# Query-weight load and fold in four pieces, and one layer-norm step placed earlier, in a one-core Perceiver layer

## The chip, the cores and the metric

One core of one Trainium2 chip runs the whole program. The metric is the device time of one execution in microseconds (us); lower is better. TensorE (PE) does matrix products, VectorE (DVE) and ScalarE (ACT) work on elements, GpSimd (POOL) on elements as well, and SyncE (SP) issues DMAs. Each engine runs its own list of instructions in order and waits on semaphores.

## The reference

```python
# x: 16 x 64 x 256, context: 16 x 1601 x 256
x = x + cross_attention(layernorm(x), ctx, seg_id)      # latent keys and values, 16 heads, rope
x = x + self_attention(layernorm(x))
x = x + moe(layernorm(x))                               # 8 routed experts (top 2) and 2 shared ones

# in cross_attention, what the change touches:
kv_c   = kv @ W_kvc                                     # 64 wide
q_c    = layernorm(x) @ W_dq                            # 96 wide
q_nope = (q_c @ W_uq).reshape(b, lq, H, HD)             # HD = 128
k_nope = (kv_c @ W_uk).reshape(b, lk, H, HD)
scores = q_nope . k_nope + rope(q_c @ W_qr) . rope(kv_c @ W_kr)
good   = (k_ids <= seg_id) & (k_ids >= seg_id - 8)
```

## The kernel before, in words

The 1024 rows of x are eight tiles of 128 rows (two batch elements each). Cross attention runs over the tiles in a software pipeline, then self attention, then the experts. What the change touches lies in the setup, the first 25 us, and what follows it is a long stretch that PE fills.

**Folding.** Instead of expanding queries and keys to 128 per head, the kernel multiplies W_uq and W_uk of each head into one 96 x 64 matrix (`w_q[:, 0]`). PE does it once, in the loop of L1592 and L1593, 16 matrix products that the profile shows as 32, since a product of 32-bit numbers takes two passes. Before it PE runs nine products on zeros (`keep_warm`, L1321) and a small fold of two products (L1589). The weights come in one transfer of 1280 KB, L362, third in SP's list; behind it stand the two context transfers of tile 0 (L367) and the rope weights `w_q[:, 1]` (L371). SP's transfers share the 16 DMA engines with those that ACT issues: x tiles 0 and 1, the constants `consts_a`, and the segment numbers `seg_i` (L1030 to L1032).

**Tile 0 behind the fold.** On PE: the transposes of the normed rows `xT(0)` (L1316, `ps<-consts_a,xn`), `kv(0)` (L1337), `qc(0)` (L1331), one tiny product for a flag (L1602), the rope query product `y_rope(0)` (L1345, which waits for `qc_done`) and `y_lat(0)`. On DVE: `query_compressed(0)` (L623) copies the result of `qc(0)` and signals `qc_done`; L729 makes the flag `far_i`, which every engine reads before a branch (`general`, L333 to L335); `front_k(0)` (L599 to L619) and `front_rotate(0)` (L605 to L607) apply rope. The fold's result is copied by ACT (L1040). The branch guards a general path that these inputs don't take.

**The window.** On POOL three long operations, L501, L503 and L504, turn the segment numbers into the attention window `win`. They begin when DVE has converted `seg_i` (L721 to L725), and `win` is wanted only at the scores of tile 0.

**The second rows.** `normed` (L591 to L595) writes the normed rows of one tile into the single buffer `xn`: it waits for `rstd` from POOL and until PE has transposed the rows that stood there before (`xT_ps`), and runs one tensor_scalar, L594. For tile 1 it stands at L798, behind the copy `front_qt(0)` (L636) and a wait for the rest of x. PE's transposes of tile 1 wait for it. Places in the order of each engine are set by the order in which the code is written; there is no scheduler.

Of the kernel before, what the change touches and what calls it, by code (L numbers as in the profile page):

```python
# [22 lines left out]
B, LQ, D = 16, 64, 256  # L23
# [5 lines left out]
H, HD, KVC, QC, R = 16, 128, 64, 96, 64  # L29
# [63 lines left out]
def build(nc, dram):  # L93
    with ExitStack() as ctx:
        def sb(name, shape, dt=F32):
            return ctx.enter_context(nc.sbuf_tensor(name, shape, dt))

        def sem(name):
            return ctx.enter_context(nc.semaphore(name))
# [24 lines left out]
        w_shared = sb("w_shared", [P, NSH, WX])  # L124
        w_routed = sb("w_routed", [P, E, WX])

        def carve(store):

            at = [0]

            def cut(*shape):
                n = int(np.prod(shape))
                part = store[:, at[0]:at[0] + n]
                at[0] += n
                letters = "abcd"[:len(shape)]
                return part.rearrange(f"p ({' '.join(letters)}) -> p {' '.join(letters)}",
                                      **dict(zip(letters[1:], shape[1:])))
            return cut


        cut = carve(w_shared[:].rearrange("p e n -> p (e n)"))
        w_uq, w_uk, w_uv, w_o = cut(H, QC), cut(H, KVC), cut(H, KVC), cut(H, D)

        cut = carve(w_routed[:, E // 2:, :].rearrange("p e n -> p (e n)"))
        w_q = cut(2, H, KVC)[0:QC]
# [20 lines left out]
        xn = sb("xn", [P, D])  # L166
# [102 lines left out]
        names = """seg_moved tiles_sent flag_set flag_ps far_ready g_step moe_in zero_set zeroed ws_in wr_in late_in c_xn3 c_xT_ps c_xT lg_ps lg e_done  # L269
# [6 lines left out]
        xs_in = [sem(f"xs_in{q}") for q in range(3)]  # L276
        b_up_in = [sem(f"b_up_in{q}") for q in range(2)]
        b_dn_in = [sem(f"b_dn_in{q}") for q in range(2)]
        names = """wu_in wr_q_in seg_in const_in x0_in x_in wk_in wv_in wo_in aw_in ctx_in win_ready dve_step pool_step
            absorb_q_ps absorb_q absorb_k_ps absorb_k absorb_m_ps absorb_m  # L280
            mv_ready rstd_ready xn_ready xT_ps xT_done qc_ps qc_done kv_ps kv_raw ylat_ps qlat
            yrope_ps yrope_used qrope krope kT_ps kT_done qt_lo_ps qt_lo qt_hi_ps qt_hi kvx
# [1 line left out]
            bxn bT_ps bxT_done bq_ps bqm bkv_ps bk_done bv_done bs_ps bs_used bmax bsub bp_done bpt_ps  # L284
            bpt_done bo_ps bon bot_done bproj_ps x3_done out_done""".split()
        S = {n: sem(n) for n in names}

        (wu_in, wr_q_in, seg_in, const_in, x0_in, x_in, wk_in, wv_in, wo_in, aw_in, ctx_in, win_ready, dve_step, pool_step,
         absorb_q_ps, absorb_q, absorb_k_ps, absorb_k, absorb_m_ps, absorb_m,
         mv_ready, rstd_ready, xn_ready, xT_ps, xT_done, qc_ps, qc_done, kv_ps, kv_raw, ylat_ps, qlat,  # L290
         yrope_ps, yrope_used, qrope, krope, kT_ps, kT_done, qt_lo_ps, qt_lo, qt_hi_ps, qt_hi, kvx,
# [1 line left out]
         bxn, bT_ps, bxT_done, bq_ps, bqm, bkv_ps, bk_done, bv_done, bs_ps, bs_used, bmax, bsub, bp_done, bpt_ps,  # L293
         bpt_done, bo_ps, bon, bot_done, bproj_ps, x3_done, out_done) = [S[n] for n in names]

# [56 lines left out]
        def after(eng, s, count):  # L352

            if not isinstance(count, int) or count > 0:
                eng.wait_ge(s, count)
# [3 lines left out]
        def _(sp):  # L359
            sp.dma_start(w_kT[:], dram["w_kT"]).then_inc(wk_in, 16)  # L360
            sp.dma_start(w_kd[:], dram["w_kd"]).then_inc(wk_in, 16)
            sp.dma_start(w_shared[:].rearrange("p e n -> p (e n)")[:, 0:H * (QC + KVC)], dram["w_uqk"]).then_inc(wu_in, 16)  # L362

            def load_ctx(i):
                after(sp, kv_ps, i)
# [37 lines left out]
            n = NU * D // ZC  # L403
# [155 lines left out]
        def _(dve):  # L559
# [31 lines left out]
            def normed(i, count, dst, used_sem, signal, used):  # L591
                dve.wait_ge(rstd_ready, count)
                after(dve, used_sem, used)
                dve.tensor_scalar(dst[:], x_sb[:, i, :], mv[:, i, 0:1], rstd[:, bass.ds(i, 1)],  # L594
                                  ALU.subtract, ALU.mult).then_inc(signal, 1)  # L595
# [25 lines left out]
            def query_compressed(i):  # L621
                dve.wait_ge(qc_ps, i + 1)
                dve.tensor_copy(qcT[:], ps[0:QC, 1, 0:P]).then_inc(qc_done, 1)  # L623
# [70 lines left out]
            def body(i, link_, behind, more):  # L694
                maxima(i, 0)
                query_compressed(i + 1)
                if more:
                    link_(dve.bn_stats(bn[:], x_sb[:, i + 2, :]))
                divided(i, 0, link_)
                if more:  # L700
                    link_(dve.bn_aggr(mv1[:], bn[:]))
                    dve.tensor_tensor(mv[:, i + 2, :], mv1[:], eps[:], ALU.add).then_inc(mv_ready, 1)
                front_k(i + 1, link_)
                front_rotate(i + 1)
                maxima(i, 1)
                front_rotated(i + 1)
                if not behind:
                    for j in range(2):
                        dve.wait_ge(absorb_m_ps, j + 1)
                        dve.tensor_copy(w_m[:, 2 * j:2 * j + 2, :].rearrange("p j d -> p (j d)"), ps[:, 4 + j, :]).then_inc(absorb_m, 1)  # L710
                divided(i, 1, link_)
                front_qt(i + 1)
                if more:
                    normed(i + 2, 3 if isinstance(i, int) and i == 0 else 2 * i + 2, xn, xT_ps, xn_ready, i + 2)
                if behind:
                    residual(i - 1, link_)
# [6 lines left out]
            link(dve.tensor_scalar(far[:, NT:2 * NT], seg[:], 0.0, None, ALU.is_lt))  # L723
            dve.tensor_reduce(far_n[:], far[:], AX.X, ALU.max).then_inc(flag_set, 1)
            dve.tensor_scalar(seg[:], seg[:], -LOOKBACK / 2, None, ALU.add).then_inc(seg_moved, 1)  # L725

            query_compressed(0)
            dve.wait_ge(flag_ps, 1)
# [66 lines left out]
            general(dve, g_tile, None, g_clear)  # L795
            front_qt(0)
            dve.wait_ge(x_in, 16)
            normed(1, 2, xn, xT_ps, xn_ready, 1)  # L798
            body(0, link, False, True)
            body(1, link, True, True)  # L800
            base = steps[0]
# [1 line left out]
            with dve.Fori(2, NT - 2) as i:  # L803
                n = [0]
# [50 lines left out]
            with dve.Fori(2, NT - 2) as i:  # L855
                n = [0]
# [150 lines left out]
            for m in range(MF + 1, MN):  # L1007
                product(m)
                t = m - MF
                if t >= IC + 1 and t % IC == 1:  # L1010
                    g = m // IC - 1
# [8 lines left out]
            g = len(PAIRS) - 1  # L1020
# [293 lines left out]
        def _(pe):  # L1314
# [273 lines left out]
            for k in range(KT):  # L1588
                last = pe.matmul(ps[:, 6, k * R:(k + 1) * R], w_kvcT[:, k * P:(k + 1) * P], w_kr[:], start=True, stop=True)  # L1589
            last.then_inc(absorb_k_ps, 1)  # L1590
            pe.wait_ge(wu_in, 16)
            for h in range(H):  # L1592
                last = pe.matmul(ps[0:QC, 4 + h // 8, (h % 8) * KVC:(h % 8 + 1) * KVC], w_uq[:, h, :], w_uk[:, h, :],  # L1593
                                 start=True, stop=True)
            last.then_inc(absorb_q_ps, 1)
# [329 lines left out]
def laid_out(inputs):  # L1925

    a = {k: np.asarray(v) for k, v in inputs.items()}
    g = lambda n: a["L0_xattn_" + n]
    s = lambda n: a["L0_attn_" + n]
    rows = lambda w: w.reshape(KT, P, -1).transpose(1, 0, 2)  # L1930
    heads = lambda w, n: w.reshape(n, H, HD).transpose(2, 1, 0)

    def expert(gate, up, down):

        n = gate.shape[0]
        gu = np.stack([gate, up], 1).transpose(0, 3, 1, 2).reshape(n, KT, P, 2 * I).transpose(0, 2, 1, 3)
        dn = down.transpose(0, 2, 1).reshape(n, IC, P, D).transpose(0, 2, 1, 3)
        return np.concatenate([gu.reshape(n, P, -1), dn.reshape(n, P, -1)], 2)

    flat = lambda w: np.ascontiguousarray(w).reshape(w.shape[0], -1)  # L1940
    c = constants()
    c["w_router"] = flat(rows(a["L0_ffn_w_router"].T))
    pack = lambda table: np.concatenate([c[n] for n in table], 1)
    a_wo = s("Wo").reshape(NP_, 2, DH, D).transpose(0, 2, 1, 3).reshape(P, 2, D)
    return {
        "x": a["x"].reshape(T, D),
        "ctxT": a["ctx_2048"].transpose(0, 2, 1),
        "seg": a["itok_BxS_0_1023"].reshape(NT, P).T,
        "consts_a": pack(PACK_A), "consts_b": pack(PACK_B),
        "rope_c_all": c["rope_c_all"], "rope_s_all": c["rope_s_all"],  # L1950
        "w_uqk": np.concatenate([flat(heads(g("W_uq"), QC)), flat(heads(g("W_uk"), KVC))], 1),
        "w_uvo": np.concatenate([flat(heads(g("W_uv"), KVC)), flat(g("W_o").reshape(H, HD, D).transpose(1, 0, 2))], 1),
        "w_kT": np.concatenate([g("W_kvc").T, g("W_kr")], 1),
        "w_kd": np.concatenate([rows(g("W_kvc")), np.zeros((P, KT, R), np.float32), rows(g("W_dq"))], 2),
        "w_qr": g("W_qr").reshape(QC, H, R),
        "a_w": np.concatenate([flat(rows(s("Wq"))), flat(rows(s("Wk"))), flat(rows(s("Wv"))), flat(a_wo)], 1),
        "w_routed": expert(*(a["L0_ffn_" + n] for n in ("wg", "wu", "wd"))),
        "w_shared": expert(*(a["L0_ffn_" + n] for n in ("sg", "su", "sd"))).transpose(1, 0, 2),
    }
# [18 lines left out]
```

## Time and profile before

| what | value |
|---|---|
| three runs | 514.43, 515.78, 516.9 us (median 515.78) |
| profiled execution | 515.22 us |
| its span in the trace | 513.4 us |
| granted TensorE clock | full in all 40 slices |
| PE busy | 496.7 us, 97% of the span |
| DVE, ACT, POOL busy | 246.8, 184.9, 67.7 us |

The profiled execution took 1.8 us more than its span, which is what lies before the first and behind the last recorded instruction. PE is nearly always busy from 24 us on, so the time is to be found in the few places where PE waits; many of them lie in the setup.

### The profile page before, as it was taken

To read this page: it belongs to the slowest core of one execution; us is meant where nothing else is said; L and a number is where in the kernel's file an instruction comes from. 1 tells how busy PE (TensorE), PEld (TensorE's weight loads), DVE (VectorE), ACT (ScalarE), POOL (GpSimd) and SP (SyncE) were. 2 spreads that over 40 slices of the span, in tenths; PEclk is the share of its full clock that TensorE was granted. 3 is DMA by queue.
4 is the path that set the end of the run, shared out by engine and by line. 5 is a ranking of instruction groups with operands and counts; after the bars stand their busy time and mean duration, and the time that the engine had idled before them with its cause. 6 is when DMAs were issued, how large, how long until landed. Compare 5 with 4: busy or idle time off the path is not lost.

```text
span 513.4 us, 10570 instructions
## 1 busy us (share of the span) xinstructions
PE 496.7 (97%) x3878; PEld 361.3 (70%) x3878; DVE 246.8 (48%) x547; ACT 184.9 (36%) x533; POOL 67.7 (13%) x74
## 2 busy tenths in 40 slices
PE   7799999999999999998999998999999999999997
PEld 6476876876877788886788885555555555556886
DVE  1485776776766678888562221212222222222334
ACT  1367566566666544444411111212212112111110
POOL 6200000000000112132006500000000000000650
PEclk9999999999999999999999999999999999999999
DMA  7730000001990019300614162787887877852341
GB/s 224 274 138 21 1 22 20 0 20 60 357 419 4 2 41 431 146 0 1 263 48 133 72 250 67 268 289 262 317 272 270 320 262 282 311 197 83 84 121 41
DMA packets 24456, 82.05 MB, mean 160 GB/s; under 512 B 2881, under 2 KB 16513, under 8 KB 20321
## 3 DMA queue, kind: packets, MB, share of 16 engines
q1 hardware_dynamic: 21392, 73.30, 39.6%
q0 software_dynamic: 1536, 4.20, 2.6%
q10 hardware_dynamic: 1488, 4.00, 2.1%
q8 instruction: 28, 0.46, 0.3%
q14 instruction: 12, 0.09, 0.1%
HBM read 73.10 MB, written 8.39 MB: 159 GB/s over the span
## 4 chain that ended last, share of the span: by engine, by line
PE 87%; DVE 5%; issue 3%; DMA 2%; ACT 1%; POOL 0%; DVEq 0%; SPq 0%; POOLq 0%
PE ps L1812 17%; PE ps L1720 13%; PE ps L1316 12%; PE ps L1836 9%; PE ps L1732 6%; PE ps L1395 5%; PE ps L1345 5%; PE ps L1364 5%; PE ps L1487 3%; PE ps L1383 3%; DMA w_shared<-in_w_uqk 2%; PE ps L1497 1%; PE ps L1676 1%; PE ps L1337 1%; PE ps L1360 1%
## 5 line engine op out<-in xcount | busy, mean ns | idle before, releaser
L1812 PE MATMUL ps<-w_routed,xnT 128*64 x320 | 93.8, 436 | 1.6 <-DVE x_sb L969 1.6
L1720 PE MATMUL ps<-xT_all,w_shared 128*128 128x256 f32 x320 | 75.6, 380 | 0.0
L1812 PEld LDWEIGHTS ps<-w_routed,xnT 128*64 128x64 f32 x320 | 42.0, 137 | 38.4 <-issue 27.2
L1720 PEld LDWEIGHTS ps<-xT_all,w_shared 128*128 128x128 f32 x320 | 60.4, 190 | 8.3 <-issue 0.4
L1093 ACT ACTIVATE w_routed<-ps,neg_top 128x128 f32<-128x128 f32 x128 | 45.0, 378 | 15.9 <-DVE neg_top L644 15.9
L1836 PE MATMUL ps<-w_routed,hidT 128*64 x200 | 47.4, 384 | 0.0
L1812 PE MATMUL ps<-w_shared,xnT 128*64 128x384 f32 (+1 forms) x160 | 46.9, 436 | 0.0
L1812 PE MATMUL ps<-x_up,xnT 128*64 128x384 f32 (+1 forms) x160 | 46.9, 436 | 0.0
L1316 PEld LDWEIGHTS ps<-consts_a,w_routed 128*128 128x128 f32 x336 | 37.2, 141 | 13.5 <-issue 10.4
L1285 ACT COPY hidT<-ps 128x384 f32<-128x384 f32 x20 | 9.6, 479 | 100.7 <-PE ps L1316 100.7
L1258 ACT ACTIVATE sil<-ps 128x256 f32<-128x256 f32 x40 | 15.3, 384 | 84.3 <-PE ps L1720 84.2
L1316 PE MATMUL ps<-consts_a,w_routed 128*128 128x128 f32 x336 | 44.3, 276 | 1.1 <-DVE w_routed L831 0.5
L1836 PEld LDWEIGHTS ps<-w_routed,hidT 128*64 128x64 f32 x200 | 25.8, 137 | 15.0 <-issue 3.3
L1364 PEld LDWEIGHTS ps<-hid,w_routed 128*128 128x128 f32 x256 | 33.6, 192 | 1.2
L963 DVE COPY hidT<-ps 128x256 f32<-128x256 f32 x20 | 8.5, 425 | 53.4 <-PE ps L1316 53.4
L1364 PE MATMUL ps<-hid,w_routed 128*128 128x128 f32 x256 | 33.7, 275 | 0.0
L554 POOL DMA_INDIRECT x_up<-y_slots,slot_i x8 | 8.0, 995 | 182.7 <-DVE hidT L876 180.5
L644 DVE TENSOR_REDUCE neg_top<-ps 128x4 f32<-128x512 f32 x32 | 22.0, 689 | 16.5 <-PE ps L1364 16.0
L493 POOL TENSOR_TENSOR rstd<-mv,half 128x1 f32 (+1 forms) x16 | 9.1, 566 | 157.7 <-DVE mv L574 95.9
L1345 PE MATMUL ps<-w_routed 96*128 96x512 f32 x64 | 29.0, 595 | 0.3 <-issue 0.3
L1395 PE MATMUL ps<-w_routed 128*128 128x256 f32 x128 | 29.0, 379 | 0.0
L1093 ACT ACTIVATION_READ_ACCUMULATOR w_routed<-ps,neg_top 128x1 f32 x128 | 27.8, 217 | 0.0
(180 smaller groups left out, 873.6 us busy)
## 6 DMA issues: line engine op xcount, KB each, us to landing
w_routed<-in_w_routed SPq DMA_DIRECT2D x8, 1920.0 KB, 14.4
x_up<-in_w_routed SPq DMA_DIRECT2D x10, 1280.0 KB, 5.9
w_shared<-in_w_routed SPq DMA_DIRECT2D x10, 1280.0 KB, 6.4
b_down<-in_w_routed SPq DMA_DIRECT2D x10, 640.0 KB, 5.6
w_shared<-in_w_routed SPq DMA_DIRECT2D x10, 640.0 KB, 5.3
w_shared<-in_w_shared SPq DMA_DIRECT2D x1, 3840.0 KB, 12.0
w_shared<-in_w_uvo ACTq DMA_DIRECT2D x1, 2560.0 KB, 12.6
x_slots<-sil SPq DMA_DIRECT2D x16, 160.0 KB, 2.2
```

Source lines behind the costliest of these rows:

```text
L644: dve.tensor_reduce(neg_top[:, b, n], s[:, n], AX.X, ALU.min).then_inc(top_ready, 1)
L1093: last = act.activation(Pb[:, b, n, :], s[:, n, :], ACT.Exp, scale=-1.0, bias=neg_top[:, b, n:n + 1], accum_out=sums[:, b, n:n + 1])
L1316: return pe.transpose(out, src, ident[:])
L1345: last = pe.matmul(ps[:, 2 * part + c, :], qcT[:], w[:, c * 512:(c + 1) * 512], start=True, stop=True)
L1364: last = pe.matmul(at[:, n * P:(n + 1) * P], QT[:, b, h:h + 2, :], KTb[:, b, :], start=False, stop=n == 3)
L1383: last = pe.matmul(ps[KVC * h:KVC * h + KVC, 4 + 2 * b, :].rearrange("p (j t) -> p j t", t=P), kv_ext[:, b, 0:KVC], PT[:, b].rearrange("p ...
L1395: last = pe.matmul(ps[:, b, 0:D], UT[:, j, h, :], w_m[:, 2 * j + h, :], start=j == h == 0, stop=j == NP_ // 2 - 1 and h == 1)
L1487: last = pe.matmul(ps[:, b, g * P:(g + 1) * P], w[:, k, g * P:(g + 1) * P], xnT[:, k, :], start=k == 0, stop=k == KT - 1)
L1720: last = pe.matmul(ps[:, UP_BANK[m], half_ * D:(half_ + 1) * D].rearrange("p (n t) -> p n t", n=2), w_shared[:, j, at:at + P], xT_all[:, i ...
L1732: last = pe.matmul(ps[:, Y_BANK[g][n], n * D:(n + 1) * D], hidT_ring[m % 4][:, n * P:(n + 1) * P], w_shared[:, PAIRS[g][0], GU + c * D:GU ...
L1812: last = pe.matmul(ps[rows, b, 0:hi - lo], xnT[:, k, rows], w, start=k == 0, stop=k == KT - 1)
L1836: last = pe.matmul(ps[rows, 6, 0:D], hidT[:, c, rows], w, start=c == 0, stop=c == IC - 1)
```

## The change

The weights W_uq and W_uk are laid out in memory head by head, 96 and then 64 numbers for each head, so that a quarter of the buffer holds both factors of four heads. SP issues four transfers of 320 KB in place of the one, each with a semaphore of its own, and PE waits for one of them before every fourth head. On DVE `normed` of tile 1 moves from L798 to just before `query_compressed(0)`. The wait for the rest of x stays where it was. Each row of a transfer has 2560 bytes in place of 10240.

```diff
-        w_uq, w_uk, w_uv, w_o = cut(H, QC), cut(H, KVC), cut(H, KVC), cut(H, D)
+        w_uqk, w_uv, w_o = cut(H, QC + KVC), cut(H, KVC), cut(H, D)
+        w_uq, w_uk = w_uqk[:, :, 0:QC], w_uqk[:, :, QC:]
...
+        wu_in = [sem(f"wu_in{q}") for q in range(4)]
...
-            sp.dma_start(w_shared[:].rearrange("p e n -> p (e n)")[:, 0:H * (QC + KVC)], dram["w_uqk"]).then_inc(wu_in, 16)
+            for q in range(4):
+                part = slice(q * (H // 4) * (QC + KVC), (q + 1) * (H // 4) * (QC + KVC))
+                sp.dma_start(w_shared[:].rearrange("p e n -> p (e n)")[:, part], dram["w_uqk"][:, part]).then_inc(wu_in[q], 16)
...
             dve.tensor_scalar(seg[:], seg[:], -LOOKBACK / 2, None, ALU.add).then_inc(seg_moved, 1)
+            normed(1, 2, xn, xT_ps, xn_ready, 1)
 
             query_compressed(0)
...
             dve.wait_ge(x_in, 16)
-            normed(1, 2, xn, xT_ps, xn_ready, 1)
             body(0, link, False, True)
...
-            pe.wait_ge(wu_in, 16)
             for h in range(H):
+                if h % (H // 4) == 0:
+                    pe.wait_ge(wu_in[h // (H // 4)], 16)
                 last = pe.matmul(ps[0:QC, 4 + h // 8, (h % 8) * KVC:(h % 8 + 1) * KVC], w_uq[:, h, :], w_uk[:, h, :],
                                  start=True, stop=True)
...
-        "w_uqk": np.concatenate([flat(heads(g("W_uq"), QC)), flat(heads(g("W_uk"), KVC))], 1),
+        "w_uqk": flat(np.concatenate([heads(g("W_uq"), QC), heads(g("W_uk"), KVC)], 2)),
```

PE's list at the fold, before. `w_shared` is the buffer in which the two factors lie, `w_kT` the small fold's, and the names in brackets are the semaphores waited for.

```order
L1589 MATMUL ps<-w_kT 128x64 [waits wk_in]
L1589 MATMUL ps<-w_kT 128x64
L1593 MATMUL ps<-w_shared 96x64 [waits wu_in]
L1593 MATMUL ps<-w_shared 96x64 x15
L1316 MATMUL ps<-consts_a,xn 128x128 [waits xn_ready,const_in]
L1316 MATMUL ps<-consts_a,xn 128x128
```

The same place of PE's list after the change (lines are four or five further down in this file).

```order
L1593 MATMUL ps<-w_kT 128x64 [waits wk_in]
L1593 MATMUL ps<-w_kT 128x64
L1598 MATMUL ps<-w_shared 96x64 [waits wu_in0]
L1598 MATMUL ps<-w_shared 96x64 x3
L1598 MATMUL ps<-w_shared 96x64 [waits wu_in1]
L1598 MATMUL ps<-w_shared 96x64 x3
L1598 MATMUL ps<-w_shared 96x64 [waits wu_in2]
L1598 MATMUL ps<-w_shared 96x64 x3
L1598 MATMUL ps<-w_shared 96x64 [waits wu_in3]
L1598 MATMUL ps<-w_shared 96x64 x3
L1320 MATMUL ps<-consts_a,xn 128x128 [waits xn_ready,const_in]
L1320 MATMUL ps<-consts_a,xn 128x128
```

One wait for everything has become four waits with four heads behind each; nothing else moves on PE.

DVE's list where the compressed query of tile 0 is copied, before. `seg` holds the segment numbers, L623 is `query_compressed`, L729 the flag.

```order
L724 TENSOR_REDUCE far_n<-far 128x1 [waits dve_step]
L725 TENSOR_SCALAR seg<-seg 128x8
L623 COPY w_routed<-ps 96x128 [waits qc_ps]
L729 TENSOR_SCALAR far_i<-ps 1x1 [waits flag_ps]
L599 TENSOR_TENSOR hidT<-w_routed,consts_a 128x2x64 [waits kv_raw]
```

And after, where L598 is the tensor_scalar of `normed`:

```order
L728 TENSOR_REDUCE far_n<-far 128x1 [waits dve_step]
L729 TENSOR_SCALAR seg<-seg 128x8
L598 TENSOR_SCALAR xn<-x_sb,mv,rstd 128x256 [waits xT_ps,rstd_ready]
L627 COPY w_routed<-ps 96x128 [waits qc_ps]
L734 TENSOR_SCALAR far_i<-ps 1x1 [waits flag_ps]
L603 TENSOR_TENSOR hidT<-w_routed,consts_a 128x2x64 [waits kv_raw]
```

The tensor_scalar stands ahead of the copy of the compressed query, of the flag and of the rope work, and it waits for PE's transposes of tile 0.

## Rows read from the trace of the kernel before

**Rows 1.** The page's part 4: who holds the chain that ended last.

```profile
PE 87%; DVE 5%; issue 3%; DMA 2%; ACT 1%; POOL 0%; DVEq 0%; SPq 0%; POOLq 0%
```

**Rows 2.** The chain in the first 40 us: start us, us, what.

```profile
1.99 8.10 DMA w_shared<-in_w_uqk
10.13 2.94 PE ps L1593 x32
15.54 1.97 PE ps L1345 x4
17.53 1.22 DVE w_routed L605
21.54 1.30 PE ps L1316 x10
24.00 0.42 DVE xn L594
24.50 0.41 PE ps L1316 x2
```

**Rows 3.** Timeline of the setup: start us, us, engine, line, operation [idle before].

```profile
7.04 0.17 DVE L721 CAST seg<-seg_i 128x8 f32<-128x8 int32 x1 [1.03 <-DMA seg_i<-in_seg]
7.85 0.66 PE L1589 MATMUL ps<-w_kT 64*128 64x64 f32 x4
9.88 1.89 POOL L503 TENSOR_TENSOR xT_all<-xT_all 128x1024 f32<-128x1024 f32 x1
11.87 3.65 POOL L504 TENSOR_SCALAR w_routed<-xT_all 128x1024 bf16<-128x1024 f32 x1
12.90 0.39 PE L1316 MATMUL ps<-consts_a,xn 128*128 128x128 f32 x2
15.15 0.29 DVE L623 COPY w_routed<-ps 96x128 f32<-96x128 f32 x1 [7.38 <-PE ps L1331]
15.42 0.27 DVE L599 TENSOR_TENSOR hidT<-w_routed,consts_a 128x128 f32<-128x128 f32 x1
19.98 1.22 DVE L632 TENSOR_TENSOR w_routed<-w_routed 128x1024 f32<-128x1024 f32 x1
22.86 1.23 DVE L636 COPY w_routed<-ps 128x1024 f32<-128x1024 f32 x1 [1.65 <-PE ps L1316]
```

**Rows 4.** DMAs issued at 1.75, 2.94 and 3.46 us: issue to landing, last column.

```profile
seg_i<-in_seg ACTq DMA_DIRECT2D x1, 4.0 KB, 5.3
w_routed<-in_ctxT SPq DMA_DIRECT2D x1, 128.0 KB, 8.4
w_routed<-in_w_qr SPq DMA_DIRECT2D x1, 384.0 KB, 8.9
```

**Rows 5.** DMA traffic from 3 to 4 us, then 7 to 8 us.

```profile
DMA packets 220, 0.37 MB, mean 367 GB/s; under 512 B 26, under 2 KB 120, under 8 KB 220
...
DMA packets 41, 0.42 MB, mean 420 GB/s; under 512 B 0, under 2 KB 0, under 8 KB 0
```

**Rows 6.** DMA queues from 6 to 7 us: packets, MB, share of 16 engines.

```profile
q1 hardware_dynamic: 34, 0.35, 87.2%
q10 hardware_dynamic: 2, 0.00, 0.1%
```

**Rows 7.** DVE's tensor_scalar beside POOL, timeline at 177 and 233 us.

```profile
176.96 1.90 POOL L524 TENSOR_TENSOR w_routed<-w_routed,smx 128x1024 f32<-128x1024 f32 x1 [3.54 <-DVE smx L672]
178.36 0.65 DVE L594 TENSOR_SCALAR xn<-x_sb,mv,rstd 128x256 f32<-128x256 f32 x1
...
233.42 2.31 DVE L866 TENSOR_SCALAR x_up<-x_sb,mv,rstd 128x256 f32<-128x256 f32 x2
233.58 2.00 POOL L524 TENSOR_TENSOR w_routed<-w_routed,smx 128x1024 f32<-128x1024 f32 x1 [4.61 <-DVE smx L672]
```

**Rows 8.** Line L866 alone: ns min/median/max.

```profile
L866 DVE TENSOR_SCALAR x_up<-x_sb,mv,rstd x8: 404/406/1990, 233.4 to 248.6; 128x256 f32<-128x256 f32 x8
```

**Rows 9.** Line L335, the branch behind the flag, on PE, ns min/median/max.

```profile
L335 PEldq COMPARE_BRANCH  x1: 4832/4832/4832, 16.5 to 16.5; - x1
```

More of the change, by code:

```diff
@@ L278, in build @@
         b_dn_in = [sem(f"b_dn_in{q}") for q in range(2)]
-        names = """wu_in wr_q_in seg_in const_in x0_in x_in wk_in wv_in wo_in aw_in ctx_in win_ready dve_step pool_step
+        names = """wr_q_in seg_in const_in x0_in x_in wk_in wv_in wo_in aw_in ctx_in win_ready dve_step pool_step
             absorb_q_ps absorb_q absorb_k_ps absorb_k absorb_m_ps absorb_m
@@ L286, in build @@
         S = {n: sem(n) for n in names}
-        (wu_in, wr_q_in, seg_in, const_in, x0_in, x_in, wk_in, wv_in, wo_in, aw_in, ctx_in, win_ready, dve_step, pool_step,
+        wu_in = [sem(f"wu_in{q}") for q in range(4)]
+        (wr_q_in, seg_in, const_in, x0_in, x_in, wk_in, wv_in, wo_in, aw_in, ctx_in, win_ready, dve_step, pool_step,
          absorb_q_ps, absorb_q, absorb_k_ps, absorb_k, absorb_m_ps, absorb_m,
```

## The prediction

> **What bounds the kernel.** I read the chain of waits first, then its first 25 us in order of time, then the timeline of the engines there, and last the queues of the DMAs. PE holds 87% of the chain [rows 1], so what the setup wins or loses reaches the end almost undivided: from 24 us on every step hangs on an earlier one, and the later loads are issued by signals of that same work. In the setup the chain [rows 2] is: the weights landing at 10.09, the fold of 32 passes to 12.90, where the transposes of tile 0 begin, y_rope(0) at 15.54, rope on DVE from 17.53, PE again at 21.54, the norm of the second rows at 24.00 and its transposes at 24.50. The reader is to see that two pieces stand in the open: the fold behind the last byte, and the norm behind the copy L636.
>
> **The norm leaves its old place.** L636 runs from 22.86 for 1.23 us, to 24.09 [rows 3]; the transposes of tile 1 begin at 24.50 [rows 2]. Without L594 between them they begin some 0.05 us behind the copy, at 24.14. I take 0.36 us, with bounds 0.32 and 0.42 (the norm's own duration). PE goes on with the scores of tile 0, whose first half needs nothing later than that copy. The wait for the rest of x stays, and those rows are issued earlier if anything.
>
> **The fold, taken alone.** PE leaves the nine warm-up products at 7.85 and the small fold at 8.51 [rows 3], before which the first quarter can't start. The fold's pace is 2.77 us (10.13 to 12.90) for 32 passes, 0.087 each. Bound by PE it ends at 8.5 + 2.8 = 11.3. Bound by the landing it ends 8 passes, 0.7 us, behind the last quarter. That quarter lands at 10.09 if the size of a packet costs nothing. By the rows of mixed smaller packets, 367 GB/s against 420 with 10 KB ones [rows 5], 1.31 MB take 3.57 us in place of 3.12, so it lands at 10.5. The fold then ends between 10.8 and 11.3; I take 11.25, since PE is the later in both, and xT(0) begins 1.65 us earlier. Three more issues on SP, 0.5 us each as between those at 2.94 and 3.46 [rows 4], push the context and the rope weights back by 1.5 us in SP's list. They were queued behind the big transfer anyway: the context landed at 2.94 + 8.4 = 11.3 and is wanted at 11.45, the rope weights at 3.46 + 8.9 = 12.4 [rows 4] and are wanted near 13.9. If both slip by 1.5 us, kv(0) starts at 12.8 and 1.3 us of the 1.65 are gone, in the case where they would count.
>
> **What the new place costs.** The norm now stands ahead of query_compressed(0) on DVE. It is released when xT(0) ends, 0.39 us behind its start: at about 11.65. It looks free, as DVE idles 7.38 us before L623 [rows 3]. It is not free if POOL is in a long operation. In the trace DVE's tensor_scalar from buffer to buffer doesn't run beside one. At 178.36 it stood 0.65 us and ended at 179.01, while POOL's L524 ran to 178.86. At 233 us two of them took 2.31 us together, the longer 1.99 where the others take 0.41, and ended at 235.73 with L524 ending at 235.58 [rows 7, 8]. Both ended 0.15 us behind POOL. The Trainium skill says the same as a rule (SBUF — State Buffer, "Who interferes with whom"): VectorE in a two-port mode and GpSimd exclude each other for a whole instruction, and the first to issue holds the ports. This case's trace agrees, with 1.99 against 0.41 us, and the rule speaks against this place.
>
> Here POOL computes the window: L503 from 9.88 to 11.77, L504 from 11.87 for 3.65 us, to 15.52 [rows 3]. A norm released at 11.65 would wait out L503 and slip in before L504. One released after 11.87 waits for the end of L504, E, and ends at E + 0.15; L623 follows (0.29), then y_rope(0) 0.10 later as before (15.44 to 15.54): at E + 0.54. The flag and with it PE's branch, 4.83 us from 16.5 [rows 9], stand behind the same copy and move alike. So the question is when POOL starts. Its chain hangs on seg_i, which landed at 7.04, and L504 begins 4.83 us and ends 8.48 us after that landing. seg_i is 4 KB and took 5.3 us [rows 4]; from 6 to 7 us its queue moved its last 2 packets while the other queue moved 34 of 10 KB [rows 6]. One such packet holds an engine for about 16/41 = 0.39 us [rows 5]. With quarters the packets at the head are 2.5 KB, about 0.1 us each, so the stragglers should come sooner. Bounds for the landing are 6.0 (no packet of the big transfer in its way) and 7.1 (nothing gained). I take 6.55, midway but nearer the row's end than a full gain would be. L504 then runs from 11.4 to 15.0, and the norm, released at 11.65, is 0.25 us too late for the gap.
>
> **The sum.** y_rope(0) starts at 15.0 + 0.54 = 15.54, just where it did: the fold's 1.65 us are all spent in the wait. The 0.36 of the norm stay. From the profiled 515.22 us that is 514.9. The profiled execution lies 0.56 below the median 515.78; I start midway, at 515.5, and get 515.1. With seg_i landing from 6.0 to 7.1, E goes from 14.5 to 15.6, and the gain from 0.9 to -0.2: 514.6 to 515.7.
>
> **Rivals.**
> First, the norm slips in before L504. It does if seg_i still lands after about 6.85, or if the fold ends 0.25 us sooner. Then y_rope moves by the 1.65 us of the fold and the sum is 1.65 + 0.36 = 2.0: 513.5 us. For it speaks that the gap of the row before, 11.77 to 11.87, lies behind my 11.65; against it that four semaphores and a slower stream can only make PE later, and that seg_i should land sooner. The rope work L599 would then be due at 13.6, during L504. The row before can't say whether it would be held as well: it began at 15.42, 0.1 before POOL's end, and took its 0.27. If held, it ends 2 us later than due and rope on DVE (from 17.53, less 1.65) starts at 16.5 in place of 15.9. L632 ended at 21.20 and PE resumed at 21.54, so half of that is slack, and the gain is 1.7 to 2.0. The Trainium skill has that too (same page and section): with two SBUF inputs VectorE contends with a GpSimd instruction that reads SBUF. By it the rope work is held; no run here shows it yet.
>
> Second, POOL's L504 doesn't hold DVE at all, since the rows that show a hold are of another operation, L524, with two inputs. Then all is gained whatever seg_i does: 2.0 us, 513.5.
>
> Third, slower. L504 ends later than 15.4, because seg_i lands later than 6.9 and the norm misses the gap all the same, for a last quarter that lands after 10.7. Then y_rope starts at E + 0.54: at 16.06 with E as before, half a microsecond late, against 0.36 gained. That is 0.15 us lost; with seg_i at 7.5, half a microsecond behind its row, 0.6 lost: 515.6 to 516.1. For it: four transfers where there was one. Against it: smaller packets share an engine more evenly.
>
> Fourth, the weights in quarters land no sooner than the whole and the norm's old place was covered by something else (the second half of ACT's copy for the scores): nothing changes, 515.5.
>
> **How the numbers follow.** Forecast 0.50; the first rival 0.26; the second 0.08; the third 0.10; the fourth 0.06. The likeliest gives 515.1, its own range is 514.3 to 516.0 with the runs' scatter of a microsecond. The range reaches to the first two rivals: 513.0 to 516.2. This kernel's measurement can tell 0.5% from nothing, 2.6 us, a time under 513.2. Only the first two rivals come near, with 2.0 us; scatter carries them over in about 3 of 10 cases, 0.10, and 0.03 I add for a PE branch that ends sooner by a microsecond with x landed before it. Slower by 2.6 us nothing here reaches; 0.03 for what I have not seen. The same: 0.84.
>
> **What would show it.** The tensor_scalar L598 with a duration near 3 us and an end 0.15 us behind POOL's L504; seg_i's landing before 6.8; the fold ending near 11.3 without a wait between quarters; y_rope(0) within 0.5 us of 15.54; the transposes of tile 1 0.05 us behind the copy. L598 at 0.4 us with y_rope near 13.9 means the first or second rival, told apart by POOL's clock at that moment. A fold that ends after 12 makes the transfer's part of this wrong.

## The result, and the profile after

The changed kernel took 515.29 us (median of 21 runs, 512.07 to 516.48), the kernel before 517.59 us in 21 runs of the same series (514.02 to 522.35). The ratio is 0.9943, with a 95% interval from 0.9921 to 0.9965: 0.6% faster, 1.8 to 4.1 us. The kernel before had shown 515.78 in three runs; with more runs its median moved up by 1.8 us, over twice the 0.7 us that the change was forecast to bring. The profiled execution of the changed kernel took 514.32 us with a span of 512.5, 0.9 us less than before.

So there are two questions: why the setup became faster at all, where the forecast had let its gain vanish, and why the runs show more than the 0.9 us of the two profiles.

The chain of the changed kernel in the setup: start us, us, what ("issue" is time in which the engine waited for nothing that the profile shows).

```profile
3.42 7.41 DMA w_shared<-in_w_uqk
10.87 0.89 PE ps L1598 x8
11.76 0.23 PE ps L1320 x2
12.12 1.13 PE ps L1341 x8
14.23 1.97 PE ps L1349 x4
16.23 1.23 DVE w_routed L609
20.54 1.30 PE ps L1320 x10
23.23 0.41 PE ps L1320 x2
26.07 0.77 issue
27.23 0.89 PE ps L1341 x8
```

Against [rows 2]: y_rope(0) starts at 14.23 in place of 15.54, PE resumes behind the branch at 20.54 in place of 21.54, the transposes of tile 1 start at 23.23 in place of 24.50. The gain is 1.31, 1.00 and 1.27 us at these places. It is 0.9 at the end.

The timeline of the changed kernel, same columns as [rows 3]:

```profile
7.01 0.17 DVE L725 CAST seg<-seg_i 128x8 f32<-128x8 int32 x1 [0.97 <-DMA seg_i<-in_seg]
8.01 2.57 PE L1598 MATMUL ps<-w_shared 128*96 128x64 f32 x24
10.87 0.89 PE L1598 MATMUL ps<-w_shared 128*96 128x64 f32 x8 [0.29 <-DMA w_shared<-in_w_uqk]
11.60 0.39 PE L1320 MATMUL ps<-consts_a,xn 128*128 128x128 f32 x2
11.85 3.65 POOL L508 TENSOR_SCALAR w_routed<-xT_all 128x1024 bf16<-128x1024 f32 x1
12.10 0.94 DVE L598 TENSOR_SCALAR xn<-x_sb,mv,rstd 128x256 f32<-128x256 f32 x1 [4.35 <-PE ps L1320]
13.85 0.29 DVE L627 COPY w_routed<-ps 96x128 f32<-96x128 f32 x1 [0.81 <-PE ps L1335]
14.12 0.27 DVE L603 TENSOR_TENSOR hidT<-w_routed,consts_a 128x128 f32<-128x128 f32 x1
14.69 0.29 DVE L623 TENSOR_TENSOR hidT<-hidT,w_routed 128x128 f32<-128x128 f32 x1
```

The reader is to see the sixth row. The moved norm was released at 12.10, behind the start of POOL's window operation at 11.85, just as forecast. It was held, but for half a microsecond: 0.94 in place of 0.41 us. It ended at 13.04, 2.5 us before POOL's row does, and left DVE idle for 0.81 us before the copy of the compressed query. The last two rows, rope work with two inputs, ran inside POOL's operation at their usual 0.27 and 0.29.

### The profile page after: what moved, and what is told of

Its sections match the earlier page's. It is cut to its first block, busy times and chain, and to the rows that moved or that the text cites. A ratio compares the mean times of both kernels' runs of the same rounds, so it can differ in the third digit from the quotient of the medians.

```text
span 512.5 us, 10574 instructions
## 1 busy us (share of the span) xinstructions
PE 496.6 (97%) x3878; PEld 361.1 (70%) x3878; DVE 247.4 (48%) x547; ACT 185.1 (36%) x533; POOL 67.6 (13%) x74
## 4 chain that ended last, share of the span: by engine, by line
PE 87%; DVE 6%; issue 3%; DMA 1%; ACT 1%; SPq 0%; POOL 0%; DVEq 0%; POOLq 0%
PE ps L1817 17%; PE ps L1725 13%; PE ps L1320 12%; PE ps L1841 9%; PE ps L1737 6%; PE ps L1399 5%; PE ps L1349 5%; PE ps L1368 5%; PE ps L1491 3%; PE ps L1387 3%; DMA w_shared<-in_w_uqk 1%; PE ps L1341 1%; PE ps L1501 1%; PE ps L1681 1%; PE ps L1364 1%
```

## The experiments

The mean granted clock of each execution turned out to matter, so the table gives it for all kernels. "Full" are executions with a mean clock of at least 0.9985, "low" those of at most 0.9905. The three rows of the kernel before belong to the three groups of experiments below.

| kernel | runs | median | at full clock | low clock | ratio to before (95%) |
|---|---|---|---|---|---|
| before, first group | 29 | 517.20 | 514.75 (8 runs) | 11 | |
| before, second group | 35 | 517.05 | 514.44 (7) | 11 | |
| before, third group | 29 | 516.69 | 515.01 (8) | 11 | |
| the change | 21 | 515.29 | 512.71 (5) | 1 | 0.9943 (0.9921 to 0.9965) |
| e1_split | 12 | 514.95 | 513.59 (2) | 1 | 0.9938 (0.9907 to 0.9969) |
| e2_norm | 12 | 517.83 | 515.33 (1) | 6 | 1.0006 (0.9968 to 1.0043) |
| e4_late_aw | 12 | 514.95 | 512.95 (2) | 0 | 0.9942 (0.9909 to 0.9974) |
| e5_warm13 | 12 | 516.81 | 515.68 (6) | 1 | 0.9986 (0.9957 to 1.0014) |
| e6_fill | 12 | 515.64 | 515.46 (9) | 0 | 0.9975 (0.9945 to 1.0005) |
| e7_all_first | 12 | 518.30 | 514.92 (3) | 5 | 1.0015 (0.9977 to 1.0054) |
| e8_two | 12 | 515.03 | 513.71 (5) | 2 | 0.9962 (0.9928 to 0.9995) |
| e9_wide5 | 12 | 513.83 | 513.00 (3) | 2 | 0.9954 (0.9925 to 0.9983) |
| e10_wide5_fill2 | 12 | 513.48 | 513.04 (7) | 0 | 0.9949 (0.9922 to 0.9976) |
| e11_before_wide | 12 | 515.89 | 515.39 (5) | 2 | 0.9987 (0.9956 to 1.0018) |

### Each part alone: e1_split and e2_norm

e1_split is the change with this undone:

```diff
-            normed(1, 2, xn, xT_ps, xn_ready, 1)
 
             query_compressed(0)
...
             dve.wait_ge(x_in, 16)
+            normed(1, 2, xn, xT_ps, xn_ready, 1)
             body(0, link, False, True)
```

> The change with the second norm back in its old place, so only the four transfers are left. In the profile of the changed kernel xT(0) starts 1.3 us earlier (12.90 to 11.60), and y_rope(0) too. If the two parts add up: the transposes of tile 1 begin near 23.6 (before 24.50, changed 23.23), gain against the kernel before about 0.9 us less what PE gives back in its branch, 515.78 becomes some 515. If the norm was what held the gain back, this kernel would be faster than the changed one, with y_rope(0) before 14.2. If the whole 0.57% of the changed kernel comes from the transfers, the ratio is 0.994 here.

e2_norm is the kernel before with that edit alone, the other way round.

> The kernel before with the second norm alone moved. The weights land as before, xT(0) ends at 13.3, the norm is released during POOL's L504 (11.87 to 15.52). If POOL holds the ports to its end, as I predicted, the norm ends at 15.67, y_rope(0) starts at 16.06 in place of 15.54 and the kernel is 0.1 us slower. If the hold is shorter, as the changed kernel's 0.94 us suggests, the norm ends by 14.3, y_rope(0) stays at 15.54, the transposes of tile 1 come 0.3 to 0.4 us earlier, and the ratio is 0.999.

The transfers carry all that the runs can tell: 0.9938 alone, 0.9943 with the norm. The norm alone is at 1.0006. In its profile the moved norm ran inside POOL's operation and was not held at all:

```profile
13.35 3.66 POOL L504 TENSOR_SCALAR w_routed<-xT_all 128x1024 bf16<-128x1024 f32 x1
...
14.24 0.41 DVE L594 TENSOR_SCALAR xn<-x_sb,mv,rstd 128x256 f32<-128x256 f32 x1 [4.99 <-PE ps L1316]
```

By my forecast it would have waited to 17.16. It ended at 14.65. I had expected y_rope(0) at 15.54; it started at 16.37, since the weights, in one transfer as before, landed at 10.92 in this execution and not at 10.09. The profile of e1_split was the first with another clock. It has the times of the changed kernel up to y_rope(0) (14.12), and then, in PE's pause before the branch target, this (start:end, us, busy times with counts of PE, its weight loads, DVE, ACT and POOL, granted clock, DMA share, GB/s):

```profile
18.00:19.00 1.00, 0.00 (x0) 0.00 (x0) 0.96 (x2) 0.84 (x1) 0.00 (x0) 1.00 0.97 251
19.00:20.00 1.00, 0.00 (x0) 0.00 (x0) 0.79 (x1) 0.00 (x0) 0.00 (x0) 0.74 0.82 322
20.00:21.00 1.00, 0.79 (x4) 0.82 (x5) 0.00 (x0) 0.09 (x1) 0.00 (x0) 0.50 0.99 410
26.00:27.00 1.00, 1.00 (x8) 0.96 (x8) 0.21 (x1) 0.00 (x0) 0.00 (x0) 0.85 1.00 430
```

PE stands idle from 17.8; its clock goes to half, 1.2 GHz, during the 20th microsecond and is back near 26.3. Over the executions of the kernel before, a mean clock lower by 0.01 goes with 4.5 us more (fitted over 29 runs, 514.5 at full clock). Most of its scatter of 9 us goes with the clock, and that is the second thing in which the two kernels differ: 11 of 29 executions before are at low clock, and one of 21 after.

A mean clock is a sum over the whole execution, and it doesn't say where the clock fell. In this profile it fell at a second place, behind short pauses of PE (1.59 and 0.48 us, near 235 and 237 us), far from anything that the change touches:

```profile
237.00:238.00 1.00, 0.74 (x7) 0.74 (x8) 0.94 (x3) 0.69 (x2) 0.00 (x0) 0.97 0.00 0
238.00:239.00 1.00, 1.00 (x7) 1.00 (x6) 0.93 (x5) 0.11 (x1) 0.06 (x1) 0.50 0.00 0
```

The profiles of e5_warm13 and e8_two show a drop at the same place. So the mean of 0.989 of this execution has nothing to do with the fold.

### How long POOL holds: e3_probe

Sixteen more tensor_scalars on DVE, ahead of the moved norm, whose results are not used:

```diff
+            for _ in range(16):
+                link(dve.tensor_scalar(y_sb[:], x_sb[:, 0, :], 2.0, 1.0, ALU.mult, ALU.add))
             normed(1, 2, xn, xT_ps, xn_ready, 1)
```

> The changed kernel with 16 more tensor_scalars on DVE (256 columns, buffer to buffer, results unused) ahead of the second norm, so that one is always running or waiting from 7.8 us on, beside POOL's three window operations. If any POOL operation holds them for its whole length: one or two run at each seam between POOL operations, and the rest last 1.9 or 3.6 us. If the two-input tensor_tensors hold and the tensor_scalar with bf16 result does not: about 2 us each beside the first two, and 0.4 to 0.9 us beside the third, some six of them. If the hold is only the first microsecond of the third, one of 1 us and then 0.41 each.

Its timeline, POOL's three operations and five of the sixteen, each asked for in a window of its own:

```profile
7.65 1.90 POOL L505 TENSOR_TENSOR xT_all<-consts_a,seg 128x1024 f32<-128x1024 f32 x1 [1.72 <-DVE seg L729]
7.73 1.96 DVE L731 TENSOR_SCALAR y_sb<-x_sb 128x256 f32<-128x256 f32 x1
...
9.62 1.89 POOL L507 TENSOR_TENSOR xT_all<-xT_all 128x1024 f32<-128x1024 f32 x1
...
11.61 3.72 POOL L508 TENSOR_SCALAR w_routed<-xT_all 128x1024 bf16<-128x1024 f32 x1
...
11.70 1.10 DVE L731 TENSOR_SCALAR y_sb<-x_sb 128x256 f32<-128x256 f32 x1
...
13.16 0.29 DVE L731 TENSOR_SCALAR y_sb<-x_sb 128x256 f32<-128x256 f32 x1
...
14.47 1.00 DVE L731 TENSOR_SCALAR y_sb<-x_sb 128x256 f32<-128x256 f32 x1
15.83 0.29 DVE L731 TENSOR_SCALAR y_sb<-x_sb 128x256 f32<-128x256 f32 x1
```

Beside the tensor_tensor one tensor_scalar lasts as long as POOL's operation, 1.96 us, as in [rows 7]. Beside POOL's tensor_scalar with a bf16 result there are three stretches. From 11.70 to 12.80 DVE is held. From 12.83 to 14.43 five tensor_scalars run at 0.29 each. One that begins at 14.47 is held to 15.47, 0.14 us behind the end of POOL's row. I had expected a hold at the start or none, not the second one. With this the changed kernel's 12.10 to 13.04 is a release 1.19 us behind POOL's start, and the probe's was 1.19 as well (11.61 to 12.80). e2_norm fits: with an end no sooner than 13.35 + 1.19 = 14.54, the norm, begun at 14.24, took its usual 0.41 and ended at 14.65. Two more profiles measure the same holds on the norm itself. In e9_wide5 it began 0.57 us behind POOL's start, took 0.62 and ended again 1.19 behind it. In e7_all_first it began 0.45 us before POOL's end, in the second hold, and ended 0.16 behind it:

```profile
10.99 3.65 POOL L508 TENSOR_SCALAR w_routed<-xT_all 128x1024 bf16<-128x1024 f32 x1
14.19 0.61 DVE L598 TENSOR_SCALAR xn<-x_sb,mv,rstd 128x256 f32<-128x256 f32 x1 [7.29 <-PE ps L1320]
```

### The streaming of the fold: e7_all_first, e8_two

e7_all_first keeps layout, transfers and norm, but PE waits for all before the first head:

```diff
+            for q in range(4):
+                pe.wait_ge(wu_in[q], 16)
             for h in range(H):
-                if h % (H // 4) == 0:
-                    pe.wait_ge(wu_in[h // (H // 4)], 16)
```

> The changed kernel (four transfers, layout, norm moved), but PE waits for all four transfers before the first head. PE then pauses from 8.0 to 10.8 as in the kernel before, and the fold ends near 13.6. If the gain is the streaming of the fold, all of it is gone: xT(0) at 13.6, executions with a clock of 0.984 to 0.990 are back, median 517 to 518, ratio 1.000 to 1.002. If layout or smaller transfers gain by themselves, the ratio stays below 0.998.

No gain is left that the runs can tell: 1.0015, and 5 of 12 executions are at low clock again. Its profile has PE idle for 2.33 us, and the fold behind it:

```profile
7.97 0.66 PE L1593 MATMUL ps<-w_kT 64*128 64x64 f32 x4
10.95 2.90 PE L1598 MATMUL ps<-w_shared 128*96 128x64 f32 x32 [2.33 <-DMA w_shared<-in_w_uqk]
13.69 0.39 PE L1320 MATMUL ps<-consts_a,xn 128*128 128x128 f32 x2
```

e8_two has transfers of 12 and of 4 heads:

```diff
-            for q in range(4):
-                part = slice(q * (H // 4) * (QC + KVC), (q + 1) * (H // 4) * (QC + KVC))
+            for q, (lo_, hi_) in enumerate(((0, 12), (12, H))):
+                part = slice(lo_ * (QC + KVC), hi_ * (QC + KVC))
...
-                if h % (H // 4) == 0:
-                    pe.wait_ge(wu_in[h // (H // 4)], 16)
+                if h in (0, 12):
+                    pe.wait_ge(wu_in[h // 12], 16)
```

> The changed kernel with two transfers, of 12 heads and of 4, in place of four of 4. SP issues the context 0.95 us earlier than in the changed kernel (3.89), so that kv(0) waits less for it (12.12 there). The first transfer lands later, near 9.5, and PE folds 12 heads in 2.1 us: the fold ends near 12.3 if bound by that, against 11.6. If earlier landing of context matters more, xT(0) and kv(0) start before 11.9. Pause on PE from 8.0 to 9.5: by the clock theory some executions of 0.987 return. I expect 0.5 to 1.5 us slower than the changed kernel, ratio 0.996 to 0.998.

I was wrong on the landing. The fold ran without a pause from 8.82 to 11.75, so 12 heads had landed by 8.8 where I had said 9.5. The transposes of tile 0 began at 11.58 and kv(0) at 11.81 without a wait for the context, y_rope(0) at 14.22, the same as with four. Two transfers do the work of four in the setup. The intervals don't tell the two kernels apart; 513.71 against 512.71 at full clock rests on five runs each.

### Other loads out of the way: e4_late_aw

```diff
             load_ctx(1)
+            load_ctx(2)
             sp.dma_start(consts_b[:], dram["consts_b"]).then_inc(moe_in, 16)
             sp.dma_start(w_routed[:, E // 4, 0:4 * KT * D], dram["a_w"]).then_inc(aw_in, 16)
-            with sp.Fori(2, NT) as i:
+            with sp.Fori(3, NT) as i:
```

> The changed kernel with the constants for the experts and the self-attention weights (1.25 MB together, wanted at 150 us) issued behind the context of tile 2, near 28 us, in place of 16 us. In the changed kernel's profile PE's branch lasts 5.1 us and PE stands 0.77 us in the middle of qc(1), both at code loads. If these loads wait behind the weights' traffic, the branch shrinks by 0.3 to 1 us and the pause by up to 0.8: 0.5 to 1.5 us faster than the changed kernel. If the code load has its own pace, nothing changes.

0.9942 against 0.9943: no change that the runs can tell, though with intervals of 1.7 us to either side they don't exclude half a microsecond. In its profile PE resumed behind the branch at 20.02, with the other loads not yet issued (28.70); the branch lasted 4.75 us in place of 5.11, and the pause in qc(1) was gone. But e8_two, with the loads in their old place, has 4.85 us and no pause either. So nothing speaks for this traffic as the cause, and a small share of it stays open.

### Filling PE's pauses: e5_warm13, e6_fill

e5_warm13 is the kernel before with `WARM_UP = 13`.

> The kernel before with 13 warm-up products in place of 9, which fill PE's pause of 1.6 us between the small fold (8.51) and the weights (10.13) and end before the weights land. If the pause is why some executions of the kernel before have a mean granted clock of 0.984 to 0.990 (11 of 29, 519.3 to 522.5 us), those executions vanish, the median falls from 517.2 to about 515.5, and the fastest stay at 513.5 to 514.5. If the clock has nothing to do with that pause, the spread stays and the ratio is 1.000.

e6_fill is the changed kernel with six products on zeros:

```diff
             y_lat(0)
+            pe.wait_ge(far_ready, 1)
+            keep_warm(6)
```

> The changed kernel with six products on zeros behind y_lat(0), in PE's pause before the branch target (17.9 to 20.5). 13 of 21 executions of the changed kernel have a mean clock of 0.992 or 0.993 and 515.5 us, five have a full one and 512.7; in two profiles the clock drops to half at 19.3 or 19.7 us, in that pause. If the pause brings the drop, nearly all executions now have a full clock and the median is 512.8 to 513.3, ratio to the kernel before 0.991. If the filler only delays the branch, 0.5 to 2 us slower than the changed kernel. If the drop is not tied to pauses, no change.

Both did to the clock what the two expectations say that filled pauses would do: one low execution of 12 where the kernel before has a third, and nine of 12 at full clock where the changed kernel has five of 21. Both lost the time again at full clock: 515.68 against 514.44 in the same group, and 515.46 against 512.71. The profiles show one place. PE stops in the middle of a group of products, with nothing that it waits for. In e5_warm13, e6_fill and the changed kernel:

```profile
25.76 0.39 PE L1364 MATMUL ps<-hid,w_routed 128*128 128x128 f32 x2
27.32 0.83 PE L1364 MATMUL ps<-hid,w_routed 128*128 128x128 f32 x6 [1.17 <-issue]
```

```profile
24.01 0.94 PE L1368 MATMUL ps<-hid,w_routed 128*128 128x128 f32 x7
26.89 0.27 PE L1368 MATMUL ps<-hid,w_routed 128*128 128x128 f32 x1 [1.94 <-issue]
```

```profile
25.69 0.38 PE L1335 MATMUL ps<-xnT,w_kd 128*96 128x128 f32 x2
26.85 0.38 PE L1335 MATMUL ps<-xnT,w_kd 128*96 128x128 f32 x2 [0.77 <-issue]
```

The stop lies behind pass 2 of qc(1) in the changed kernel and in the one before. With four more products, that is eight passes, it lies eight passes earlier; with six more, twelve passes earlier. So it sits at a fixed distance from the start of PE's program, to within a pass (in e7_all_first it lies behind pass 1 of qc(1)). A queue of the kind "instruction" moved one packet of 0.02 MB two to three microseconds before it ended (24 to 25 us in the changed kernel, 25 to 26 before). I take it for a load of code; no run tests that. Its end is tied to the branch: in the seven profiles that show a stop it ended 6.0 to 6.6 us behind the moment when PE resumed at the branch target, and in e4_late_aw and e8_two, where PE came to the place 6.3 us or more behind that moment, there is none. So a PE that comes to the place sooner waits there the longer. Where the stop falls decides its price too. In the scores, DVE's maxima, ACT's exponentials and the copies of the keys behind them come later, and y_rope(1) with them.

### The same fill without more instructions: e9_wide5, e10_wide5_fill2, e11_before_wide

A product of 512 columns, the zeros read twice, fills twice the time in one instruction:

```diff
+            def keep_warm_wide(n, b=7):
+                for _ in range(n):
+                    pe.matmul(bank(b).rearrange("p (r t) -> p r t", r=2), zeros[:, 0:P],
+                              zeros[:, 0:2 * P].unsqueeze(1).to_broadcast([P, 2, 2 * P]), start=True, stop=True)
...
-            keep_warm(WARM_UP)
+            keep_warm(1)
+            keep_warm_wide(4)
```

This is e9_wide5. e10_wide5_fill2 adds `keep_warm_wide(2, 4)` behind `y_lat(0)`. e11_before_wide is the kernel before with `keep_warm(5)` and `keep_warm_wide(4)`.

> The changed kernel with the nine warm-up products of 256 columns as one of 256 and four of 512: the same columns in four instructions fewer. In the changed kernel's profile PE stands 0.77 us in the middle of qc(1), and with 4 or 6 more products (the two kernels with added fillers) it stands 1.17 and 1.94 us some 8 and 13 passes earlier in the program, ending near 26.9 to 27.3. If that pause is a load of code that falls at a fixed place of the program, it now falls 8 passes later, in or behind kv(1), and PE reaches it after 26.9: the pause is gone, 0.5 to 0.8 us faster than the changed kernel, 512.0 at full clock, median 514.6. If the pause is something else, no change. The scatter by the clock stays.

> The last kernel with two products of 512 columns on zeros behind y_lat(0), 1.7 us in PE's pause before the branch target (17.9 to 20.4), still two instructions fewer than the changed kernel. By both theories together (clock drops come from that pause, the code load falls at a fixed place): nearly all executions at full clock, the code pause no longer than 0.5 us and behind the scores, median 512.5 to 513.0, ratio 0.991, faster than both kernels. If the filler costs what the six did (515.5 at full clock), the code theory is wrong.

> The kernel before with warm-up of five products of 256 and four of 512 columns: the length of 13, which fills the pause before the weights, in the nine instructions of before. The one with 13 instructions had fewer slow-clock executions but was 1.2 us slower at full clock (515.7 against 514.5). If that was the code load moved into the scores, it is now gone: 514.5 at full clock, executions with a clock under 0.9905 (11 of 29 and 11 of 35 of the kernel before) nearly gone, median 515.0 to 515.8, ratio 0.996 to 0.997. If it stays at 515.7 at full clock, filling the pause costs time in another way.

e10_wide5_fill2 is faster than the kernel before (0.9949, interval 0.9922 to 0.9976), as the change is. Its filler covers the pause, and the clock stays:

```profile
17.37 1.72 PE ps L1329 x4
19.09 0.77 issue
19.86 1.30 PE ps L1320 x10
...
25.18 0.44 PE ps L1340 x4
25.61 0.22 PE ps L1346 x2
25.84 0.21 issue
26.05 0.94 PE ps L1346 x6
```

The load of code now costs 0.21 us and falls behind pass 2 of kv(1), four passes later than in the changed kernel, as two products fewer ask for. No execution had a mean clock under 0.995, and the range is the narrowest of all, 512.7 to 515.5. At full clock it stands at 513.04 against the change's 512.71, so the shift of the code load didn't show as a gain there; nor did it in e9_wide5 (513.00), where I had expected 512.0. The profile of e9_wide5 has no stop, but its clock fell at 20.4 us, so PE came to the place late anyway. Both ratios lie inside the change's interval, and the kernels ran on different chips: that it beats the change is not shown.

e11_before_wide gave a part of what I expected. At full clock it took 515.39 us and not 514.5, which is 0.4 more than the kernel before in the same group (515.01), where e5_warm13 had 1.2 more; the median, 515.89, and the ratio, 0.9987, missed my ranges, and 2 of 12 executions were low. With five to eight executions at full clock on a side I can't tell what is left from nothing. Its profile shows the pause before the weights from the inside. The warm-up ended at 8.44, only 0.6 us later than before (e5_warm13: at 9.17). Its products on 256 columns fell from 0.63 to 0.38 us already between 4 and 5 us, in e5_warm13 between 5 and 6. So the pause was not filled, and this is what it can cost (columns as above; then the chain):

```profile
10.00:11.00 1.00, 0.45 (x5) 0.45 (x6) 0.00 (x0) 0.00 (x0) 1.00 (x1) 1.00 0.76 143
11.00:12.00 1.00, 1.00 (x10) 1.00 (x8) 0.00 (x0) 0.00 (x0) 0.92 (x2) 0.53 0.22 74
12.00:13.00 1.00, 1.00 (x8) 1.00 (x8) 0.00 (x0) 0.00 (x0) 1.00 (x1) 0.50 0.01 4
```

```profile
10.55 4.97 PE ps L1599 x32
15.52 0.43 PE ps L1316 x2
```

PE had waited 1.45 us for the weights. The clock fell to half at about 11.1, half a microsecond behind the start of the fold, and the fold took 4.97 us where it takes 2.94 at full clock [rows 2]. The transposes of tile 0 began 2.6 us later than in [rows 3]. In the same profile it fell a second time, near 24.7, at the pause before the branch target. Two drops in one execution gave the mean clock of 0.99 here, as two drops at other places gave 0.989 in e1_split. This is the one profile with a drop at the fold.

## Why the prediction was right, and where it was not

The range, 513.0 to 516.2, holds the time, and so does the range of the likeliest case. Most of the chance was on a difference too small to tell, and the measured one is at that bound: 0.6% where I had drawn it at 0.5%. That 515.1 lies so near the measured 515.29 is luck. I started from 515.5 where the kernel before has 517.59, 2.1 us too low, and forecast a gain of 0.4 where 2.3 were measured, and the two errors cancel. The mechanism of the forecast is wrong in one step and lacks another.

**The norm, 0.36 us.** Its transposes began 0.14 us behind the copy, not 0.05: 0.27 us gained. Right in kind; e2_norm can't tell it from nothing. What was gained there seems to be lost again a little later: from PE's restart behind the branch to the stop in qc(1) the changed kernel took 5.53 us in place of 5.81, but the stop ended 6.31 behind the restart in place of 6.14.

**The fold, 1.65 us.** The last quarter landed at 10.83, where I had said 10.5 at the latest, and PE waited 0.29 us for it. My 10.5 started from one landing, 10.09. In the other profiles with a single transfer it came at 9.91, 10.51 and 10.92, and the last of four quarters at 10.07 to 10.86 in all. So the quarters cost nothing that these profiles can tell, and my row was an early one. xT(0) began at 11.60, 1.30 us earlier and not 1.65. The context made kv(0) wait to 12.12; it was queued 1.4 us later, as said. It cost no more, since ACT's copy of the folded weights stood in the way as well.

**"Waits for the end of L504, E, and ends at E + 0.15".** This is the step that failed. The release came behind the start of L504, as forecast, though seg_i landed at 7.0 and not at 6.55. (DVE took up seg_i at 7.04, 8.34, 8.51 and 8.70 in the profiles with one transfer, at 5.87 to 7.23 in those with two or four: that it comes sooner with smaller transfers was right, and again my row was an early one.) But L504 is no L524. The rows that I had were all of a tensor_tensor, and there the hold lasts to the end. e3_probe shows two holds of 1.1 and 1.0 us with 1.6 us free between them. The moved norm lost 0.5 us, all of it in DVE's idle time, and y_rope(0) moved by 1.31 us. In e6_fill the norm was released at 11.76, ahead of POOL's start at 12.07, and y_rope(0) came at 14.22 all the same: the hold cost nothing. The second rival, "L504 doesn't hold DVE at all", comes nearest, and had 0.08. The rule of the Trainium skill that I named (SBUF — State Buffer, "Who interferes with whom"), that the first to issue holds the ports for the whole instruction, agrees with [rows 7] and not with e3_probe; here the measurement decides. The same page's second rule, that two SBUF inputs contend with a GpSimd instruction that reads SBUF, is not borne out by this trace: L603 took its 0.27 us at 14.12, and L623 its 0.29 at 14.69, inside the last microsecond of POOL's operation, in which the probe's tensor_scalars and the norm of e7_all_first were held.

**What PE gave back.** From y_rope(0) on, 1.31 us became 0.83 at kv(1). The branch lasted 5.11 us in place of 4.83, and the stop of the code load 0.77 in place of 0.34. I had no term for either. Over all profiles but the probe's, PE resumed 5.7 to 6.7 us behind the start of y_rope(0), so 0.3 us between two of them is within their scatter.

**The clock, missing altogether.** I had read "full in all 40 slices" from one execution and took it for a property of the kernel. It is one outcome of several. At full clock the kernels stand at 514.75 and 512.71, 2.0 us apart (fitted over all executions, 514.46 and 512.79, 1.7 us). The means over all executions are 517.61 and 514.80, 2.8 us apart. The rest, about 1.1 us, goes with the clock: executions at low clock are frequent before and rare after. Kernels that let PE idle before the fold (before, e2_norm, e7_all_first) had 44 low executions of 117; those that stream it in four transfers without fillers (the change, e1_split, e4_late_aw) had 2 of 45, and e8_two and e9_wide5 together 4 of 24. The likely reason is a drop at the fold, behind the pause that streaming removes; it is argued from these counts and from the one profile of e11_before_wide, since no profile of the kernel before shows it. Why full-clock executions differ by 2.0 us and the two profiles by 0.9 is shown in part. In the four profiles at full clock there of kernels that wait for all weights, y_rope(0) started at 15.54, 16.37, 15.35 and 16.32; in the seven that stream them, without the probe, at 13.70 to 14.27. That is 1.1 to 2.7 us, with 1.8 between the means, where the pair that I compared shows 1.31. Besides, the profiled execution of the changed kernel, 514.32, is the slowest of its five at full clock.

## What to carry to other kernels

A load that feeds a block of products is worth cutting even where the saved time looks small, because the pause that it removes can also cost a clock drop; judge it by many executions with their granted clock, not by one profile. A hold between two engines is a property of the pair of instructions: a row of another operation on the same engine is a bound, not a price. Fillers on PE were not free here even in a pause: each instruction shifted the point at which PE stopped, so try few wide ones; that these are faster is not shown. One landing read from one profile is a draw: the same single transfer came between 9.9 and 10.9 us.

## What the runs showed of the hardware

- POOL's tensor_scalar of 128x1024 with a bf16 result holds DVE's buffer-to-buffer tensor_scalar from its start to 1.19 us behind it and again in its last microsecond (from 0.86 us before its end at the latest), with 1.6 us free between (e3_probe, and the norm in e9_wide5 and e7_all_first). DVE's tensor_tensors of 128x128 with two inputs were not held in that last microsecond (0.29 us). POOL's tensor_tensor of the same size holds it to the end, 1.96 us.
- PE's clock fell to half half a microsecond behind a pause of 1.45 us before the fold (e11_before_wide). At the pause before the branch target it fell 1.7 to 2.9 us after PE had stopped (e1_split, e3_probe, e4_late_aw, e8_two, e9_wide5, e11_before_wide), and near 236 to 238 us behind pauses of 1.59 and 0.48 us (e1_split, e5_warm13, e8_two). Other executions kept full clock through the same pauses.
- PE's branch took 4.0 to 5.5 us in all profiles, where SP's and POOL's took 0.05. A stop at a fixed place of PE's program follows, for 0.21 to 1.94 us, which ends 6.0 to 6.6 us behind PE's restart; where PE comes to the place later than that, there is none. An instruction queue moved a packet two to three microseconds before each end.
